# A four-layer graph kernel: the product with C in high and low parts, tensors moved into used-up weights, new orders

## The reference

```python
# layer 0, eight heads of 32 columns (k, j), per batch b
Xp = einsum('bnd,hdk->bhnk', X, Wp) + bp
Xc = einsum('bhnk,hjk->bhnj', Xp, C)              # the product with C
attn = tanh(A * einsum('bhnj,bhmj->bhnm', Xc, Xp))
out = relu(attn @ Xp)
# layer 1: hypergraph convolution with W1 (256 -> 512), relu, layer norm, the same with W2 (512 -> 256)
# layer 2: softmax-like transition from adj * exp(leaky_relu(si + sj)), two hops of it, three weights Wk
# layer 3: gate from degrees, QK = sigmoid(xg @ Wqk.T + bqk), attn from (QK @ QK.T) * adj,
#          relu((attn @ xg) @ Wl.T + bl + xg @ Wr.T)
```

## Time and profile before

| | |
|---|---|
| runs | 1861.01, 1861.93, 1866.42 us (median 1861.93) |
| profiled execution | 1861.08 us, of which the span from first to last instruction is 1859.3 us |
| PE busy | 1792.6 us (96% of the span) |
| DVE / ACT / POOL busy | 1567.4 (84%) / 1245.6 (67%) / 920.2 us (49%) |
| mean granted TensorE clock | 0.986 |
| DMA | 100.06 MB, mean 54 GB/s |

### The profile page before, as it was taken

The page is one execution under the profiler, slowest core; times in us unless marked ns, Lnnn a source line. Parts: engine busy times, 40 slices in busy tenths (PEclk is TensorE's granted clock), DMA queues, the critical chain, the costliest instruction groups (busy, mean ns, idle before and its releaser), DMA issues.

```text
span 1859.3 us, 43155 instructions
## 1 busy us (share of the span) xinstructions
PE 1792.6 (96%) x14600; PEld 1571.5 (85%) x14600; DVE 1567.4 (84%) x4572; ACT 1245.6 (67%) x2576; POOL 920.2 (49%) x1873
## 2 busy tenths in 40 slices
PE   5799999999999999999999999999999999999985
PEld 4688888888888888888888888888888888888874
DVE  4678888888888888888888888888888888888874
ACT  4566667677677677676667667767767767767653
POOL 2335545544545555554554554554554455555443
PEclk7999999999999999999999999999999999999998
DMA  4111111111211211111111111111111121111100
GB/s 153 38 44 55 49 56 55 57 48 55 64 45 52 63 47 55 58 46 56 58 47 58 55 47 58 55 53 51 55 59 47 53 63 47 55 58 47 32 29 29
DMA packets 99676, 100.06 MB, mean 54 GB/s; under 512 B 8320, under 2 KB 90368, under 8 KB 99200
## 3 DMA queue, kind: packets, MB, share of 16 engines
q1 hardware_dynamic: 99456, 97.29, 16.7%
HBM read 80.48 MB, written 16.78 MB: 52 GB/s over the span
## 4 chain that ended last, share of the span: by engine, by line
PE 94%; DVE 2%; issue 1%; ACT 1%; POOL 1%; DMA 0%; DVEq 0%; ACTq 0%; SPq 0%; POOLq 0%
PE psum L983 56%; PE psum L992 5%; PE psum L1046 4%; PE psum L1062 4%; PE psum L1122 3%; PE psum L1038 3%; PE psum L1101 3%; PE psum L1189 3%; PE psum L1032 3%; PE psum L1196 3%; PE psum L1087 3%; PE psum L1204 2%; PE psum L1144 1%; PE psum L1174 0%; PE psum L1176 0%
## 5 line engine op out<-in xcount | busy, mean ns | idle before, releaser
L412 ACT ACTIVATE x<-res,shift,rstd 128x256 f32<-128x256 f32 x384 | 208.8, 593 | 106.9 <-DVE res L721 106.9
L300 POOL TENSOR_TENSOR var_eps<-mean_var,eps 128x2 f32<-128x2 f32 x192 | 42.3, 221 | 407.9 <-DVE mean_var L628 407.9
L305 POOL TENSOR_TENSOR rstd<-var_eps,minus_half 128x2 f32<-128x2 f32 x256 | 179.2, 700 | 20.1
L983 PE MATMUL psum<-wk_hi,xT_hi 128*128 128x258 f32 (+1 forms) x512 | 185.8, 363 | 3.1 <-DVE xT_lo L616 3.1
L636 DVE TENSOR_TENSOR masked<-psum,adjT 128x512 f32<-128x512 f32 x256 | 164.0, 684 | 17.7 <-PE psum L1046 17.7
L300 POOL TENSOR_TENSOR var_eps<-mean_var,eps_quarter 128x2 f32<-128x2 f32 x64 | 12.4, 194 | 327.3 <-DVE mean_var L628 327.3
L983 PE MATMUL psum<-wk_hi,xT_lo 128*128 128x258 f32 (+1 forms) x512 | 174.3, 340 | 0.0
L983 PE MATMUL psum<-wk_lo,xT_hi 128*128 128x258 f32 (+1 forms) x512 | 173.8, 339 | 0.0
L424 ACT ACTIVATE z<-hid_relu,hid_bias,hid_rstd 128x512 f32<-128x512 f32 x128 | 97.5, 809 | 91.5 <-POOL hid_bias L361 91.5
L983 PE MATMUL psum<-w_hi,zT_hi 128*128 128x256 f32 x512 | 144.4, 282 | 2.1 <-DVE zT_lo L616 1.1
L621 DVE BATCH_NORM_STATS2 stats<-res 128x6 f32<-128x256 f32 x384 | 143.4, 416 | 2.3
(11 more groups left out here) (193 smaller groups left out, 6339.3 us busy)
## 6 DMA issues: line engine op xcount, KB each, us to landing
adjT<-in_adj_t SPq DMA_DIRECT2D x256, 128.0 KB, 2.5
xt_in<-in_xt SPq DMA_DIRECT2D x64, 256.0 KB, 3.5
x<-in_x SPq DMA_DIRECT2D x64, 256.0 KB, 2.7
out<-wts SPq DMA_DIRECT2D x64, 256.0 KB, 2.2
wts<-in_adj SPq DMA_DIRECT2D x64, 128.0 KB, 2.1
wts<-in_w SPq DMA_DIRECT2D x1, 1028.0 KB, 6.9
wts<-in_w SPq DMA_DIRECT2D x1, 1024.0 KB, 9.6
wts<-in_w SPq DMA_DIRECT2D x1, 769.0 KB, 5.2
```

The lines of the kernel that those rows point to most:

```text
L305: pool.tensor_tensor(rstd[k][:, :], var_eps[k][:, :], minus_half[:, :], ALU.pow) \
L412: last = act.activation(xs[k + 1][:, g, :], res[k][:, g, :], ACT.Identity, scale=rstd[k][:, g:g + 1], bias=shift[k][:, g:g + 1])
L983: last = pe.matmul(dst, a, r, start=b == 0 and j == 0, stop=b == len(lhs) - 1 and j == 2)
```

## The change

1. The product with C becomes a split product. `xpT` is read twice from PSUM by ACT (`xpT`, as before, and `xpT_hi` in the rounded type), POOL makes `xpT_lo`, `c_hi` and `c_lo` are made once, and PE issues six products in place of two.
2. `x3`, `res2`, `e_pos` and `e_neg` have no memory of their own any more, they live in `wts2`, whose contents are used up after the preparation of layer 2's weights. Once each, ACT and DVE wait for that preparation.
3. All banks are dealt out anew, and the orders of all five engines. On PE: `xcT` now stands between `y1_0` and `y1_1`; the scores `att_0` to `att_3` come ahead of `conv` and `prop`; both `hop1_0` and `hop1_1` are at the head of the next turn; `rz_1` comes after `gram` and `hid_1`; `mix` after `xp`. On DVE the masks of a pair, `alpha`, `hop1`'s evacuation and `pxT_lo` stand at the end of a turn, where they were at the head of the next (so `on[1]` became `on[0]`; between which other steps they lie is what counts). On ACT `z` stands at the end of a turn, where it was first in the next. On SP the weights of layers 2, 1 and 3 are loaded in turn 0, ahead of `x0` and `adjT0`.

PE's order in a full turn is now: hop1_0, hop1_1, pxT, qkT, hop2, rz_0, hid_0, gram, xT2, hid_1, rz_1, headsT, y0_0, y0_1, heads, xp, mix_0, mix_1, y12_0, xpT, zT_0, zT_1, y12_1, si, y1_0, xcT, y1_1, att, conv, prop, xgT.

POOL's order: y0_bias, qk, edge_0, rstd2, s_lo, xT0_lo, x1_rest, hid_rstd, r_bias, si_diag, xpT_lo, rstd0, rstd3, rstd1. ACT's order around the product: gate, y12_read_0, zT_hi_0, xpT and xpT_hi, zT_hi_1, x3, e_pos and e_neg, xcT_read, x1, y12_read_1.

```diff
 TENANTS = [
-    ("hop1_1", 5, 5, "hop1_read_1"), ("pxT", 1, 2, "pxT_lo"), ("qkT", 0, 6, "qk_tanh"), ("hop2", 5, 5, "hop2_read"),
...
+    ("hop1_0", 3, 5, "hop1_read_0"), ("hop1_1", 4, 5, "hop1_read_1"), ("pxT", 6, 2, "pxT_lo"),
+    ("qkT", 1, 6, "qk_tanh"), ("hop2", 5, 5, "hop2_read"), ("rz_0", 4, 6, "z3_lo_0"), ("hid_0", 3, 2, "hid_read_0"),
...
+    ("y1_1", 7, 2, "y1_read_1"), ("att_0", 6, 0, "masked_0"), ("att_1", 4, 0, "masked_1"),
+    ("att_2", 1, 0, "masked_2"), ("att_3", 0, 0, "masked_3"), ("conv", 2, 2, "res1"), ("prop", 7, 1, "node_r"),
...
+        late2 = wts2[:, 0:3 * G * D].rearrange("p (a g d) -> p a g d", a=3, g=G)
+        xs = [sb("x0", [P, G, D]), sb("x1", [P, G, D]), sb("x2", [P, G, D]), late2[:, 0, :, :], late3[:, 0, :, :]]
...
+        xpT_hi, xpT_lo = sb("xpT_hi", [P, NC, G, P], F32R), sb("xpT_lo", [P, NC, G, P], F32R)
+        c_hi, c_lo = sb("c_hi", [P, NC, P], F32R), sb("c_lo", [P, NC, P], F32R)
...
-        e_pos, e_neg = sb("e_pos", [P, G, P]), sb("e_neg", [P, G, P])
+        e_pos, e_neg = late2[:, 2, :, 0:P], late2[:, 2, :, P:]
... (GpSimd)
+                if on[0]:
+                    wait(pool, "xcT", p[0])
+                    wait(pool, "xpT_read", n[0])
+                    pool.tensor_tensor(xpT_lo[:, :, :, :], xpT[:, :, :, :], value(xpT_hi[:, :, :, :]), ALU.subtract) \
+                        .then_inc(sem("xpT_lo"), 1)
... (ScalarE)
+                    act.activation(xpT[:, :, :, :].rearrange("p c g n -> p (c g n)"), ps("xpT"), ACT.Copy)
+                    hi(xpT_hi[:, :, :, :].rearrange("p c g n -> p (c g n)"), ps("xpT"), "xpT_read")
... (TensorE)
                 if on[0]:
                     if t.first(0):
-                        pe.wait_ge(sem("w_0"), 32)
-                    wait(pe, "xpT_read", n[0])
+                        pe.wait_ge(sem("c_lo"), 1)
+                    wait(pe, "xpT_lo", n[0])
                     claim("xcT", t)
                     for c in range(NC):
-                        last = pe.matmul(ps("xcT")[:, c * G * P:(c + 1) * G * P], c_bd[:, c, :],
-                                         xpT[:, c, :, :].rearrange("p g n -> p (g n)"), start=True, stop=True)
-                    last.then_inc(sem("xcT"), 1)
+                        split_product(ps("xcT")[:, c * G * P:(c + 1) * G * P], [(c_hi[:, c, :], c_lo[:, c, :])],
+                                      [(xpT_hi[:, c, :, :].rearrange("p g n -> p (g n)"),
+                                        xpT_lo[:, c, :, :].rearrange("p g n -> p (g n)"))],
+                                      "xcT" if c == NC - 1 else None)
+                if on[2]:
+                    y1_of(1, t, n[2])
+                if on[0]:
+                    wait(pe, "xcT_read", n[0])
+                    claim("att_0 att_1 att_2 att_3", t)
+                    scores0_of(0)
+                    scores0_of(1)
```

More of the change, by code:

```diff
@@ L31 @@
 TENANTS = [
[10 rows of a table removed]
[9 rows of a table added]
+    ("xgT", 5, 5, "xg_lo"),
 ]
@@ L362, in turn @@
                         .then_inc(sem("hid_rstd"), 1)
+                if on[6]:
+                    if t.first(6):
+                        pool.wait_ge(sem("w_3"), 32)
+                    wait(pool, "rz_read_1", n[6])
+                    pool.tensor_tensor(rz3[:, :, 0:D], rz3[:, :, 0:D], rows(bl_bc), ALU.add).then_inc(sem("r_bias"), 1)
                 if on[4]:
@@ L667, in turn @@
-                if on[4]:
-                    layer_stats(1, n[4])
-                if on[1]:
-                    mask(0, n[1], p[1])
-                    mask(1, n[1], p[1])
-                if on[6]:
-                    wait(dve, "qkT", p[6])
-                    wait(dve, "rz_1", p[6])
-                    wait(dve, "xg_hi", n[6])
-                    lo(xg_lo[:, :, :, :].rearrange("p c g n -> p (c g n)"), ps("xgT"),
-                       value(xg_hi[:, :, :, :]).rearrange("p c g n -> p (c g n)"), "xg_lo")
@@ L914, in turn @@
                     lo(wk0_lo[:, :, :], wk0_f[:, :, :], value(wk0_hi[:, :, :]), "wk0_lo")
+                if on[0]:
+                    mask(2, n[0], p[0])
+                if on[5]:
+                    wait(dve, "qkT", p[5])
+                    wait(dve, "rz_1", p[5])
+                    wait(dve, "xg_hi", n[5])
+                    lo(xg_lo[:, :, :, :].rearrange("p c g n -> p (c g n)"), ps("xgT"),
+                       value(xg_hi[:, :, :, :]).rearrange("p c g n -> p (c g n)"), "xg_lo")
@@ new lines, in turn @@
+                if on[4]:
+                    wait(dve, "hop2_read", p[4])
+                    wait(dve, "hop1_1", n[4])
+                    sums, _ = both("hop1_0", "hop1_1", slice(D, D + 1))
+                    dve.tensor_scalar(row_s[:, :].unsqueeze(2), sums, 1e-12, None, ALU.add).then_inc(sem("rows_0"), 1)
+                    wait(dve, "rows_0", n[4])
+                    dve.reciprocal(row_r[:, :], row_s[:, :]).then_inc(sem("rows_1"), 1)
+                    wait(dve, "hop2", p[4])
+                    wait(dve, "y12_read_1", n[4])
+                    wait(dve, "rows_1", n[4])
+                    _, in_order = both("hop1_0", "hop1_1", slice(D, D + 1))
+                    for g in range(G):
+                        at = g if in_order else G - 1 - g
+                        dve.scalar_tensor_tensor(out=hop1[:, g, :], in0=ps(f"hop1_{g}")[:, 0:D],
+                                                 scalar=row_r[:, at:at + 1], in1=y12[:, g, 0:D],
+                                                 op0=ALU.mult, op1=ALU.add).then_inc(sem(f"hop1_read_{g}"), 1)
@@ L1064, in turn @@
                     last.then_inc(sem("pxT"), 1)
-                if t.first(2):
-                    pe.wait_ge(sem("beta_bc"), 1)
-                    claim_once("y1_0", t)
-                    for k in range(NK):
-                        last = pe.matmul(ps("y1_0")[:, 0:D], beta_bc[:, k, :], w2_raw[:, k, :], start=k == 0, stop=k == NK - 1)
-                    last.then_inc(sem("beta_turned"), 1)
                 if on[6]:
@@ L1082, in turn @@
                                       "qkT" if j == NC - 1 else None)
+                if t.first(2):
+                    pe.wait_ge(sem("beta_bc"), 1)
+                    claim_once("y1_0", t)
+                    for k in range(NK):
+                        last = pe.matmul(ps("y1_0")[:, 0:D], beta_bc[:, k, :], w2_raw[:, k, :], start=k == 0, stop=k == NK - 1)
+                    last.then_inc(sem("beta_turned"), 1)
                 if on[5]:
```

645 lines of the change are left out of this document (317 added, 328 removed), and 14 rows, old and new, of the table TENANTS.

## The result

| | before | after |
|---|---|---|
| median, us (lowest to highest, 4 runs each) | 1861.84 (1861.01 to 1866.42) | 1833.97 (1833.93 to 1834.98) |
| ratio, 95% interval | | 0.9847 [0.9832, 0.9863] |
| profiled execution, us: time / span | 1861.08 / 1859.3 | 1834.98 / 1833.2 |
| mean granted clock | 0.986 | 0.993 |
| a full turn, from the product with C in turn 5 to that in turn 63, over 58 | 27.623 | 27.302 |

1841 was forecast, in a range of 1828 to 1858. The page of the kernel after, its busy times and the chain's shares, beside the earlier trace rows: PE is still the bound, with 20 us less; POOL has 82 us more, ACT 47, DVE 22.

A forecast was written before the change was run, and what follows sets the result against it. PE was taken to bound the middle, latency the two ends. Per full turn -0.15 - 0.33 + 0.04 + 0.08 = -0.36, times 58.5 is -21; with ends +1, 1861.1 - 21 + 1 = 1841 us, range 1828 to 1858.

The forecast's parts named there:

- Full turns: Middle of the run, bound by PE: each turn 0.36 us shorter, a period of 27.26 in place of 27.62, 58.5 times.
- The product with C: On PE, six rounded records in place of fp32: 0.72 us for 0.87, a gain of 0.15 per turn (0.12 to 0.18).
- The two waits for masks: Head of the turn on PE: the waits of hop1_1 and pxT for the masks go, -0.33 us per turn.
- `xpT_lo`: POOL's subtraction ahead of the product with C: 0.04 us late for PE, bounds nothing and 0.15.
- `qkT` behind `xg_lo`: Head of the turn: PE reaches qkT before xg_lo is ready, +0.08 us per turn, bounds 0.03 and 0.16.
- new neighbours: Rest of the new orders in a full turn: inputs found in time, number of precision switches on PE unchanged, nothing charged.
- The ends: Filling and draining of the pipeline together: +1 us, from +4 at the beginning and -3 at the end.
- The beginning: First turns: added latency for the parts, adjT0 queued behind all weights; +4 us, bounds 0 and +10.
- The end: Last turns: gram no longer waits for rz_1 and begins 1.4 us earlier; 0.7 in four turns, -3 us, bounds -6 and 0.
- The bubbles only move: Rival, full turns: hidden waits reappear elsewhere, only the product's 0.15 is left, 1853 us; chance 0.22.
- GpSimd is late: Rival, full turns: POOL held up makes xpT_lo 0.59 us late, each turn loses 0.27, 1878 us; chance 0.12.

The follow-up runs named there:

- e1: The changed kernel with the product with C back in fp32, its parts still prepared; 1846.06 us against 1860.53 for the kernel before, 0.9920.
- e2: The kernel before with the banks of att_0 and att_1 exchanged, nothing else; 1883.05 us against 1860.53, 1.0122.
- e3: The changed kernel with the scores put back behind conv and prop on PE; 1895.71 us against 1860.53 for the kernel before, 1.0187.
- e11: The changed kernel with an extra 128x256 subtraction on POOL ahead of xpT_lo from turn 8 on; 1868.70 us against 1859.01 for the kernel before, 1.0050.
- e9: The changed kernel with conv moved behind xgT on PE and two buffers for prop's SBUF copy; 1828.80 us against 1859.01 for the kernel before, 0.9836.
- e6: The changed kernel with the first loads of adjT0 and x0 ahead of the weights of layers 1 to 3; 1835.36 us, 0.9857 of the kernel before.
- e10: The changed kernel with rz_1 ahead of gram on PE only from turn 66 on; 1843.15 us against 1859.01 for the kernel before, 0.9915.
- e12: The changed kernel with the product with C in fp32, without the second read and the subtraction; 1844.76 us against 1859.01 for the kernel before, 0.9922.
- e5: The changed kernel with conv moved behind xgT on PE, nothing else; 1848.50 us against 1861.71 for the kernel before, 0.9926.
- e4: The kernel before with the split product and late tensors alone, in the old orders and banks; 1886.37 us against 1860.53, 1.0139.
- e7: The changed kernel with rz_1 ahead of gram on PE in all turns; 1928.77 us against 1861.71 for the kernel before, 1.0359.

## Why the forecast held, and where its sizes were off

*Full turns: 0.36 forecast, 0.32 measured.*
- The product with C: 0.15 forecast; 0.151 by the distances (0.865 to 0.714), 0.168 by e1. By the Trainium skill, page "FP8 and Floating Point Precision", section "TensorE Precision Notes", fp32 is four passes; three of four would be 0.87 x 3/4 = 0.65, an estimate from that page. The trace has 0.71, as the rows of before said.
- The two waits for masks: 0.33 forecast, 0.26 + 0.075 measured, with the cause shown from both kernels (e2, e3).
- `xpT_lo`: 0.04 late was forecast, on time measured, with 0.21 in hand (e11). The chain was right to the end of POOL's work. The hand-over was not: I took 0.14 to PE from a row of another pair of engines; here the product starts 0.05 after the operand is done. Counted as in the prediction, from the product's first load (889.74), the margin is 889.74 - 889.61 - 0.05 = 0.08 us; so this term could as well have gone the other way.
- `qkT` behind `xg_lo`: +0.08 forecast, 0.865 - 0.81 = 0.055 measured, and taken away by e9.
- Not foreseen, +0.11. Some 0.04 of it is the neighbours of the scores: the step ahead of the 32-row products got longer by 0.09 (`y1_1`, 1.43 to 1.52) and the one behind by 0.10 (`conv`, 0.865 to 0.967), while `prop` and `xgT`, which stood there before, got 0.09 and 0.05 back. The other 0.07 is 0.01 to 0.03 in each of `y0`, `xp`, `mix` and `y12_1`. Neither was tested by a run of its own.

I had charged "nothing" to the new neighbours. The full turns brought 18.6 us in place of 21. That the sum came so near has some luck in it: the 0.11 that I had left out was more than half paid for by the 0.065 too much that I had charged to `xpT_lo` and `qkT`.

*The ends: +1 forecast, -7.5 measured.* This is the term of the sum that failed, in both of its parts. I took one delay for the whole beginning, and I put the clock at nothing.

The beginning, forecast +4 with bounds of 0 and 10, came out at -2.5. The first `headsT` starts at 24.99 in place of 20.57, +4.4, near what I had taken, but partly by luck. The parts cost 1.83 and a later `xp` 0.70; `adjT0`, which I had thought to be the brake, was not waited for; and the other 1.9 us are PE's work, which was at the 1.2 GHz level here and not in before (see below): the transposes of `xp` up to ACT's read grew from 0.69 to 1.15 us, the product with C up to its read from 1.14 to 1.65, the scores up to the first mask from 1.26 to 2.18. The mistake is that I took the delay at the first turn for the delay of the whole beginning. The scores of turns 0 to 3, of before and then of after:

```profile
15.59 1.17 PE L1046 MATMUL psum<-xcT,xpT 32*128 32x128 f32 x32 [0.69 <-ACT xcT L472]
32.47 2.09 PE L1046 MATMUL psum<-xcT,xpT 32*128 32x128 f32 x32
56.23 1.17 PE L1046 MATMUL psum<-xcT,xpT 32*128 32x128 f32 x32
79.10 1.17 PE L1046 MATMUL psum<-xcT,xpT 32*128 32x128 f32 x32
```

```profile
19.09 2.09 PE L1067 MATMUL psum<-xcT,xpT 32*128 32x128 f32 x32 [0.69 <-ACT xcT L481]
37.80 2.09 PE L1067 MATMUL psum<-xcT,xpT 32*128 32x128 f32 x32 [0.69 <-ACT xcT L481]
60.99 1.17 PE L1067 MATMUL psum<-xcT,xpT 32*128 32x128 f32 x32
81.88 1.17 PE L1067 MATMUL psum<-xcT,xpT 32*128 32x128 f32 x32
```

After is behind by 3.5, 5.3, 4.8 and 2.8 us, and at turn 5 ahead by 2.5. The turns in which the pipeline fills are bound by latency too, and the new orders shorten them: turn 2 to turn 3 takes 20.9 us in place of 22.9, both at a granted clock of 1.00. In turn 3 the clock adds to it. The stretch from 83.5 to 90.5 us, of before and of after (the clock is the third number from the end):

```profile
83.50:90.50 7.00, 5.80 (x16) 4.55 (x16) 4.18 (x8) 3.32 (x6) 4.63 (x3) 0.51 0.23 60
```

```profile
83.50:90.50 7.00, 4.90 (x29) 4.04 (x28) 5.70 (x15) 4.43 (x7) 1.80 (x4) 1.00 0.01 2
```

Before ran there at the 1.2 GHz level. What such a stretch costs can be read off from turn 2 to turn 3 in the variants of after: e1, e6 and e10 had one of 3.4 us in it, which began between 65 and 68 us, and took 22.5, 22.3 and 22.3 us; e9, e11, e12 and after itself had none and took 20.7 to 20.9. That is 1.5 us for 3.4. e2, the kernel before but for two banks, says the same of turn 3: it was at the low level for 3.4 us of it in place of 6.8, and took 21.9 us from its scores to the next product with C where before took 23.2, 1.3 less. So of the 3.7 us that after gains on before there (19.5 for 23.2), some 2.6 to 3.0 are clock. The orders gave the rest: in turns 2, 3 and 4 about 2.0, 0.8 and 1.6.

The price is the same in turn 1, but the granted clock can mislead there. The trace has a clock only from the first change on (32.0 us in after, 11.9 in before, 46.0 in e11), and the view prints 1.00 for all that lies ahead of it. The records say otherwise. In after the rounded products of 256 columns start 0.21 apart in turn 0, where at 2.4 GHz they start 0.12 apart:

```profile
17.35 0.41 PE L1004 MATMUL psum<-xpT_hi,c_lo 128*128 128x256 f32 x1
17.57 0.41 PE L1004 MATMUL psum<-xpT_hi,c_hi 128*128 128x256 f32 x1
```

So after was at the low level until about 31 us and again from 35.4 to 45.7, and e11 without a break until 46.0. Both took 23.2 us from the scores of turn 1 to those of turn 2. e1 and e5 left the low level at 41.7 and 40.9 and took 21.3 and 21.2; e6 and e10, low until 46.8 and 47.4, took 23.7 and 23.8. So after lost about 1.9 us against e1 by 4.5 us more at the low level.

Against before, then, the clock helped after in turn 3 (2.6 to 3.0 us). It hurt it in turn 1 (7.9 us at the low level where before had 6.7: 0.5 us) and in turn 0, where before was at 2.4 GHz from 11.9 to 18.7: at most the 1.9 us above, and at least 0.6, because e12, at 2.4 GHz there but held by `adjT0` and ACT, starts its `headsT` only at 24.39. By this estimate the orders and parts by themselves made the beginning some 0.5 to 2.5 us shorter; no run separates them from the clock.

Where the low stretches fall does not look like chance alone. In the one trace of each kernel all three with the old orders (before, e2, e4) have one in turn 3, of 6.8, 3.4 and 6.8 us, and none of the eleven with the new orders has. Just ahead of it, from 79.1 to 83.5 us, PE was busy for 2.30 of 4.40 us in before; after, in the same place of its turn (81.9 to 86.3), for 3.79. That the new orders keep the clock up by leaving fewer gaps is likely from this, but argued, not shown: no run changed the gaps alone.

The end, forecast -3 with bounds of -6 and 0, was -5.0. The mechanism that I named is there: near the end PE took 1791.40 - 1787.74 = 3.66 from `hop2` to `gram` in before and takes 1784.77 - 1782.52 = 2.25 in after, the 1.4 of the forecast. In the first two turns of the drain `hop2` to `hop2` fell from 25.55 and 19.21 to 23.05 and 17.01. Before and then after:

```profile
1787.74 1.02 PE L1087 MATMUL psum<-aw_prod,alpha 128*128 128x256 f32 x4
1791.40 1.05 PE L1101 MATMUL psum<-vec 128*128 128x128 f32 x8
```

```profile
1742.46 1.03 PE L1111 MATMUL psum<-aw_prod,alpha 128*128 128x256 f32 x4
...
1765.51 1.03 PE L1111 MATMUL psum<-aw_prod,alpha 128*128 128x256 f32 x4
1767.77 1.05 PE L1129 MATMUL psum<-vec 128*128 128x128 f32 x8
...
1782.52 1.02 PE L1111 MATMUL psum<-aw_prod,alpha 128*128 128x256 f32 x4
1784.77 1.05 PE L1129 MATMUL psum<-vec 128*128 128x128 f32 x8
```

But more than half of the 5.0 is clock. Before was at the low level in four stretches here, 24.6 us in all (the first from 1776.6), after in two, 16.0 us. In the first of the two turns before had 3.4 us of it, and e4, with the same old orders and without it, took 24.00 in place of 25.55. In the second before had 3.0 us of it; e12 and e5, with the new orders and 3.4 us of it, took 18.26 and 18.37 where after took 17.01. So some 1.5 and 1.2 us of the gain are clock, and about 1 us in each of these turns is left for the orders. In the turn behind them `gram` is ahead of `rz_1`, too, and nothing was gained (18.19 before, with 0.4 us at the low level, 18.01 after). e10 supports `gram`'s place with up to 4 us, but in the new table of banks, not in the old one. Without the clock the end is some 1.3 to 2.1 us shorter (the lower figure if before's 1.8 us more at the low level in the last stretch cost as much as elsewhere), where I had taken 3.

*The rivals.* "The bubbles only move" did not happen in after, but e3, e5 and e7 show how near it lies: each moves one step of PE's list and makes the turn longer by 0.2 to 1.4 us. Of "GpSimd is late" the price was about right: with the product 0.50 late in every turn e11 is 0.29 per turn slower than before, where 0.27 was forecast for 0.59. Its cause, a collision with DVE, did not come: `xpT_lo` lies between 1295 and 1300 ns in all 41 turns from 370 to 1462 us. In before, 41 of the 43 instances of L308 that took over 300 ns lie beside the making of `xg` on DVE (L924, two SBUF inputs) and end 0.05 us behind it; 39 others, which start 0.05 us ahead of `e_exp` on DVE, also of two SBUF inputs, took 0.19 as ever. So two such inputs alone do not decide it.

## What to carry to other kernels

Here PE showed 100% busy and still held bubbles: compare the distance between two starts with that of the same form in a clean place, and look for a wait that comes once per turn. A product split into parts pays only where the chain that makes its low part fits ahead of its place in the list, so price list and product together, and measure the slack that is left. Before moving a step, list all that reads its bank and its SBUF operands and what is queued behind those readers; a second buffer in used-up weights turned a step back (e5, slower than after) into the version with the shortest turn (e9). Price the turns that fill and drain a pipeline as turns, not by the delay of the first, and look at the clock there before a difference is given to an edit: here more than half of what the drain gained was clock. Where the clock column says 1.00, check it by the distance of known products.

## What the runs showed of the hardware

- The step ahead of the 32-row products takes about 0.09 us longer than elsewhere, and the step behind them 0.05 to 0.10 (see above); moving the scores moves both.
- An operand made on POOL or DVE was used by PE 0.05 us after the end of its record (878.08 to 878.13; 896.72 to 896.77), and a product that had to wait had a first record 0.10 us dearer.
- 3.4 us at the granted 1.2 GHz level cost 1.2 to 1.6 us where the pipeline fills or drains (turns 2 and 3, and the first two turns of the drain).
- Ahead of the first change of clock on record the view prints 1.00, also where PE ran at the low level: in after the products of 256 columns start 0.213 us apart from 9.3 to 12 us, against 0.12 in full turns, and the first scores took 2.09 us and not 1.17. So the mean clocks of 0.986 and 0.993 leave these stretches out.
